# Another order of the work ahead of the second expert: a stencil step and a mixture of eight experts on one core

## The reference

```
h      = layernorm over the features * ln_g + ln_b
h_norm = (h - mean over the tokens) * rsqrt(variance over the tokens + 1e-8), per batch
hyp    = relu(emb[id] @ hyp_w1 + b) @ hyp_w2 + b
sty    = relu(hyp @ sty_w1 + b) @ sty_w2 + b      # gamma (softplus) and beta, per batch
h      = h_norm * gamma + beta
probs  = softmax(h @ router_w); the two largest of 8, rescaled, are the gates
y      = sum over 8 experts of gate_e * (relu(h @ w1_e + b1_e) @ w2_e + b2_e)
out    = x + y
```

## Time and profile before

| | |
|---|---|
| median of 3 runs | 125.39 us (124.72 to 126.44) |
| the profiled execution | 124.87 us |
| its span, first to last instruction | 123.1 us |
| TensorE busy | 113.3 us, 92% of the span |
| VectorE busy | 92.6 us, 75% |
| ScalarE busy | 74.4 us, 60% |
| GpSimd busy | 9.3 us, 8% |
| granted clock of TensorE, mean | 0.986 of full |
| bytes moved | 10.86 MB |

### The profile page before, as it was taken

How to read it: one execution, slowest core, us unless ns; L and a number is a source line. 1 busy time by engine, 2 the same in 40 slices (tenths; PEclk the granted TensorE clock), 3 DMA queues, 4 the chain that set the end, 5 groups by cost and what they waited for, 6 DMA issues and landing times.

```text
span 123.1 us, 1525 instructions
## 1 busy us (share of the span) xinstructions
PE 113.3 (92%) x509; PEld 85.8 (70%) x509; DVE 92.6 (75%) x200; ACT 74.4 (60%) x97; POOL 9.3 (8%) x18
## 2 busy tenths in 40 slices
PE   6899995994699999999999999999999999999970
PEld 2398692442247668888888888888888888888850
DVE  0588749699902839699995996799499679969781
ACT  0403525862041399788888767888887678888900
POOL 1458330000000000000000000000000000000040
PEclk9999999999679999999999999999999999999999
DMA  3999990000000007304050031005002200400004
GB/s 88 300 358 418 418 374 8 0 0 0 0 0 0 0 11 218 123 16 162 0 170 0 0 125 48 0 5 170 0 0 96 75 0 0 170 5 0 0 0 170
DMA packets 4583, 10.86 MB, mean 88 GB/s; under 512 B 800, under 2 KB 1888, under 8 KB 4576
## 3 DMA queue, kind: packets, MB, share of 16 engines
q1 hardware_dynamic: 3920, 9.93, 22.5%
q10 hardware_dynamic: 656, 0.84, 2.4%
HBM read 10.21 MB, written 0.56 MB: 87 GB/s over the span
## 4 chain that ended last, share of the span: by engine, by line
PE 82%; DVE 9%; DMA 3%; ACT 2%; issue 1%; DVEq 0%
PE zt L621 11%; PE zt L622 10%; PE zt L623 10%; PE zt L610 6%; PE aux L645 6%; PE aux L646 6%; PE aux L649 6%; PE yt L645 5%; PE yt L649 5%; PE yt L646 5%; DMA first<-d_difference_dt_ids_dram 3%; PE yt L615 3%; PE zt L539 2%; DVE st L816 1%; PE aux L602 1%
## 5 line engine op out<-in xcount | busy, mean ns | idle before, releaser
L498 ACT ACTIVATE hid_hi<-zt,pv 128x1024 fp32r<-128x1024 f32 x27 | 30.2, 1119 | 16.2 <-PE zt L623 16.1
L937 DVE TENSOR_TENSOR hid_lo<-hid,hid_hi 128x1024 fp32r<-128x1024 f32 x27 | 33.0, 1221 | 8.9 <-issue 5.4
L503 ACT ACTIVATE hid<-zt,pv 128x1024 f32<-128x1024 f32 x27 | 29.9, 1109 | 0.0
L621 PE MATMUL zt<-h_hi,ws 128*128 128x512 f32 x56 | 22.7, 406 | 0.0
L622 PE MATMUL zt<-h_hi,ws 128*128 128x512 f32 x56 | 21.8, 390 | 0.0
L623 PE MATMUL zt<-h_lo,ws 128*128 128x512 f32 x56 | 21.8, 389 | 0.0
L610 PE MATMUL zt<-h,we 128*128 128x512 f32 x16 | 8.9, 708 | 4.0 <-DVE h L845 2.8
L621 PEld LDWEIGHTS zt<-h_hi,ws 128*128 128x128 f32 x56 | 10.5, 188 | 2.9 <-issue 0.5
L622 PEld LDWEIGHTS zt<-h_hi,ws 128*128 128x128 f32 x56 | 10.5, 188 | 2.5 <-issue 0.5
L623 PEld LDWEIGHTS zt<-h_lo,ws 128*128 128x128 f32 x56 | 10.5, 188 | 2.2
L646 PE MATMUL aux<-hid_hi,ws 128*128 128x512 f32 (+1 forms) x32 | 12.0, 376 | 0.0
(11 more groups left out here) (135 smaller groups left out, 146.8 us busy)
## 6 DMA issues: line engine op xcount, KB each, us to landing
we<-in_exp_w_dram SPq DMA_DIRECT2D x8, 512.0 KB, 9.6
gate_all<-gates_dram SPq DMA_DIRECT2D x8, 512.0 KB, 3.6
f<-in_x_dram SPq DMA_DIRECT2D x2, 256.0 KB, 4.9
ft<-in_x_exchanged_dram ACTq DMA_DIRECT2D x2, 256.0 KB, 5.4
out_dram<-acc SPq DMA_DIRECT2D x1, 256.0 KB, 2.0
out_dram<-acc SPq DMA_DIRECT2D x2, 128.0 KB, 2.0
first<-d_difference_dt_ids_dram ACTq DMA_DIRECT2D x1, 136.0 KB, 3.8
gn<-in_grids_dram SPq DMA_DIRECT2D x1, 128.0 KB, 3.8
```

The costliest lines, as they stand in the source:

```text
L498: act.activation(hid_hi[:, c, :], zt[c % 2][:], ACT.Relu, bias=bias).then_inc(hi_ready, 1)
L503: act.activation(hid[:, c, :], zt[c % 2][:], ACT.Relu, bias=bias).then_inc(hid_ready, 1)
L621: pe.matmul(zt[c % 2][:, tok], w_hi, h_hi[:, tok], start=True, stop=False)
L937: v.tensor_tensor(hid_lo[:, c, :], hid[:, c, :], hid_hi[:, c, :].bitcast(F32), ALU.subtract).then_inc(lo_ready, 1)
```

## The change

Nothing that is computed changes, and no instruction is added to the real work. The order of the four lists does.

- **TensorE.** `step_cross`, `rows_b` and `columns_w` of half 1 are cut into pairs of batches. The six warm matmuls between the net's layers are gone; the pairs stand there instead. `columns_b(1)` moves behind `norm_transposed(0)`. The warm matmuls ahead of the first expert are seven instead of six, and no longer wait for `beta` first; two new ones stand ahead of the second half of expert 0. The logits of half 0 are computed ahead of these, those of half 1 behind `layer1_0(1, 0)`.
- **PSUM.** The logits go to the second half of `yt` instead of the first of `aux`, so the wait for `ld` stands ahead of `layer2_0(1, ...)` instead of expert 1's second layer.
- **ScalarE.** `relu_step(2)` runs ahead of `hyper_first`, `inverse_sd_features(0)` ahead of `style_first`, `inverse_sd_features(1)` ahead of `hidden0(0, 1)`. It takes two batches of `h` of half 1 (`H_DVE` is (2, 2) instead of (2, 4)).
- **VectorE.** `split_weights(1)` moves from behind `normalise(1)` to behind `router_start`.
- **GpSimd.** `u_b0` of half 1 comes first of the three products instead of last.

```diff
-WARM_NET = 2
-WARM_H = 6
+WARM_H = (7, 2)
-H_DVE = (2, 4)
+H_DVE = (2, 2)
-        lg_ps = aux[:, half(0)]
+        lg_ps = yt[:, half(1)]
...
             pool.wait_ge(s_ready[1], 1)
+            pool.wait_ge(f_in[1], 16)
+            pool.wait_ge(gn_in, 16)
+            product(u_b0, f, gn[:, 1, :]).then_inc(b0_ready[1], 1)
             pool.wait_ge(ft_in[1], 16)
             pool.wait_ge(gt_in, 16)
             product(u_a1, ft, gt[:, 1, :]).then_inc(a1_ready[1], 1)
             product(u_b1, ft, gt[:, 0, :]).then_inc(b1_ready[1], 1)
-            pool.wait_ge(f_in[1], 16)
-            pool.wait_ge(gn_in, 16)
-            product(u_b0, f, gn[:, 1, :]).then_inc(b0_ready[1], 1)
...
             embedded()
             relu_step(0)
+            relu_step(2)
             hyper_first()
-            relu_step(2)
             hyper_second()
+            inverse_sd_features(0)
             style_first()
-            inverse_sd_features(0)
             normalise(0)
...
             hidden0(0, 0)
+            inverse_sd_features(1)
             hidden0(0, 1)
-            inverse_sd_features(1)
             normalise(1)
...
             transposed_step(1)
+            conditioned(1)
             hidden0(1, 0)
...
             net_layer(0, pw[0:NS, EMB_AT:EMB_AT + SE], onehot[:], SE)
-            keep_warm(WARM_NET)
+            step_cross(1, 0)
             net_layer(1, pw[:, HW1_AT:HW1_AT + SH], se[:], SH)
-            step_cross(1)
+            step_cross(1, 1)
+            rows_b(1, 0, start=True)
             pe.wait_ge(p128_in, 16)
             net_layer(2, pv[:, HW2_AT:HW2_AT + SH], hyp1[:], SH)
-            keep_warm(WARM_NET)
+            rows_b(1, 1, start=True)
             net_layer(3, pv[:, SW1_AT:SW1_AT + SE], hyp2[:], SE)
-            keep_warm(WARM_NET)
+            columns_w(1, 0, final=False)
             pe.wait_ge(net_sb, 4)
...
-            rows_b(1, start=True)
-            columns_b(1)
-            columns_w(1, final=False)
+            columns_w(1, 1, final=False)
             pe.wait_ge(ident_in, 16)
             pe.wait_ge(xp_ready, BH)
             norm_transposed(0)
+            columns_b(1)
             step_transposed(0)
             rows_a(1, start=False)
 
-            pe.wait_ge(net_sb, 6)
-            keep_warm(WARM_H)
+            keep_warm(WARM_H[0])
             wait_for_h(0)
...
             step_transposed(1)
+            logits(0)
+            keep_warm(WARM_H[1])
             wait_for_h(1)
             for c in range(C):
                 if c == C - 1:
                     pe.wait_ge(acc_ready, HALVES)
                 layer1_0(1, c)
-            logits()
+                if c == 0:
+                    logits(1)
+            pe.wait_ge(ld_ready, 1)
             for c in range(C - 1):
                 layer2_0(1, c)
...
             normalise(1)
-            split_weights(1)
             moved = token_stats(1)
             scale_and_shift(1, moved)
             conditioned(1)
             input_parts()
             router_start()
+            split_weights(1)
```

More of the change, by code:

```diff
@@ L533, in net_layer, with of_pair, step_cross @@
                 pe.matmul(small[0:rows, 0:B], weights, acts, start=True, stop=True).then_inc(net_ps, 1)
-            def step_cross(n):
+            def of_pair(n, k):
+                return range(n * BH + 2 * k, n * BH + 2 * k + 2)
+            def step_cross(n, k):
                 pe.wait_ge(s_ready[n], 1)
-                for b in range(n * BH, (n + 1) * BH):
+                for b in of_pair(n, k):
                     last = pe.matmul(one_batch(zt[1], b), s_b2[:, b, :], diff, start=True, stop=True)
-                last.then_inc(rT_ready, 1)
+                if k == 1:
+                    last.then_inc(rT_ready, 1)
             def rows_a(n, start):
@@ L550, in rows_a, with rows_b @@
                         last.then_inc(df_ready, 1)
-            def rows_b(n, start):
+            def rows_b(n, k, start):
                 pe.wait_ge(b0_ready[n], 1)
[L555 to L558, removed]
+                b = n * BH + 2 * k
+                pe.matmul(pair_of(n, k), neg_half_diff2, u_b0[:, b:b + 2, :].rearrange("p b j -> p (b j)"),
+                          start=start, stop=False, skip_group_check=True)
             def columns_b(n):
@@ L564, in columns_b, with columns_w @@
                     pe.matmul(own(b), u_b1[:, b, :], neg_half_diff2, start=False, stop=False, skip_group_check=True)
-            def columns_w(n, final):
+            def columns_w(n, k, final):
                 pe.wait_ge(w_op_ready, n + 1)
-                for b in range(n * BH, (n + 1) * BH):
+                for b in of_pair(n, k):
                     last = pe.matmul(own(b), wT[:, b, :], diff, start=False, stop=final, skip_group_check=True)
-                    if final and b % 2 == 1:
-                        last.then_inc(df_ready, 1)
+                if final:
+                    last.then_inc(df_ready, 1)
             def step_transposed(n):
@@ L597, in wait_for_h, with logits @@
                     pe.wait_ge(h_act_ready, BH * (n + 1) - sum(H_DVE[:n + 1]))
-            def logits():
-                for b in range(B):
+            def logits(n):
+                for b in range(n * BH, (n + 1) * BH):
                     last = pe.matmul(lg_ps[:, b * E:(b + 1) * E], one_batch(h, b), pv[:, RW_AT:RW_AT + E],
@@ L657, in layer2 @@
                     if c == 0:
-                        if e == 1:
-                            pe.wait_ge(ld_ready, 1)
-                        else:
+                        if e > 1:
                             pe.wait_ge(yg_half, HALVES * (e - 2) + min(p, 1) + 1)
@@ L683, in _ @@
             pe.wait_ge(first_in, 16)
-            step_cross(0)
+            step_cross(0, 0)
+            step_cross(0, 1)
             rows_a(0, start=True)
             pe.wait_ge(diff2_in, 16)
-            rows_b(0, start=False)
+            rows_b(0, 0, start=False)
+            rows_b(0, 1, start=False)
             columns_b(0)
-            columns_w(0, final=True)
+            columns_w(0, 0, final=True)
+            columns_w(0, 1, final=True)
             pe.wait_ge(onehot_ready, 1)
@@ L869, in router_start @@
             def router_start():
-                v.wait_ge(logits_ready, 1)
+                v.wait_ge(logits_ready, HALVES)
                 lg = lg_ps[:, 0:B * E].rearrange("p (b e) -> p b e", e=E)
```

## The result

The changed kernel takes 119.66 us in the median of four runs (119.40 to 119.71), the kernel before 125.13 in four (124.72 to 126.44). The ratio is 0.954, 95% interval 0.947 to 0.962: faster by 4.6%. The forecast was 119.8.

The account below looks back on a forecast made before the run. TensorE bounds 82% of the span; experts 1 to 7 are fixed and only their start moves. Gains 2.1 + 0.5 + 0.5 + 1.6 + 0.85 = 5.6 us; 125.4 - 5.6 = 119.8 us, 8-in-10 range 118.6 to 121.8.

Parts of the forecast that it names:

- The block: Experts 1 to 7, from the first matmul of `layer1(1, 0)`: fixed length; only its starting moment can move.
- Part 1, the head: Up to the first L610: earlier roots and reordered TensorE queue start it at 19.1 instead of 21.21; gain 2.1 us.
- is at `norm_transposed(0)` at about 14.45: In the head, after the last net layer: TensorE has only `columns_w(1, 1)` left before half 0's transposes, formerly at 16.75.
- POOL's `u_a1`: In the head, input of `cross_operand(1)`: now POOL's second product instead of first, costing nothing or 0.1 us.
- Part 2, the split: Expert 1's weight split, moved from ahead of `token_stats(1)`: `st` of half 1 at 26.92 instead of 27.46; gain 0.5 us.
- is worth nothing: ScalarE's earlier root of half 1: no gain, as `xn` was already ahead of TensorE.
- Its new place: The split behind `router_start`, where VectorE idled 5.03 us: weights ready by 35.2, TensorE there at 37.9; no cost.
- Part 3: `h` of half 1, two tiles each on VectorE and ScalarE: 0.91 us to L610 instead of 1.43; gain 0.5 us.
- Part 4: TensorE's idle time ahead of half 1: full clock gains 1.6 us on eight passes; half of `logits` off the path, 0.85.
- The clock did not fall again: Rival ahead of half 1: light transposes and logits let the clock fall again, costing 1.6 us, 121.4 us; chance 13%.
- The head gave most of its gain: Rival that the head gives little: late products or waits lose one product's time, 121.1, or all 2.1, 121.9 us; 10%.
- The net without its six warm matmuls: Rival in the head: the level falls to half near 10 us until L610, 127.0 us, slower by 1.3%; chance 3%.

Follow-up runs that it names:

- those with the gap filled: The kernel before with eleven more warm matmuls, or 22 f32 transposes, ahead of the wait for h of half 1: medians 123.54 and 123.70 us.

## Why the prediction was right

**The block.** From L621 to the end 81.6 us in both traces. Right.

**Part 1, the head.** 1.64 us, of 2.1 forecast; 1.9 once the inputs' arrival, 0.26 us later in this execution, is taken off. The step that was too good is "is at `norm_transposed(0)` at about 14.45": TensorE came at 15.09. Of these 0.64 us, 0.26 are the inputs' arrival, the rest is the pairs. I had put a pair at 0.46 us, half of a group in a dense row. The chain of waits of the kernel after (start us, us, what) has 0.64 us for a pair of 128 x 128 between or behind the net's layers, and 0.89 for a whole group of eight passes in a row:

```profile
9.43 0.89 PE yt L574 x8
...
11.49 0.64 PE zt L543 x4
...
13.43 0.64 PE aux L574 x4
...
14.61 0.64 PE aux L574 x4
```

TensorE, not VectorE's `u_a`, still set the start of `st` (0.20 us of waiting on TensorE), if barely. The mechanism stands: TensorE's queue was the bound, and the root matters only once that is lifted, 0 alone and 0.45 behind it. POOL's `u_a1` cost nothing, `tg` did not wait.

**Part 2, the split.** `st` comes 5.64 us behind the first L610, before 6.25: 0.6, forecast 0.5. One sentence was true only of the changed kernel, that the earlier root of half 1 "is worth nothing". With the split in its old place it is worth 0.3 us: `st` comes 5.96 us behind the first L610 in the run with the split put back. So the split's move is worth 0.3 us on top of the root; without the root it would be 0.6, worked out from the same rows, which no run has by itself. Its new place is covered, as forecast: the parts of the weights are there at 33.4 and TensorE comes to them at 35.76, 2.3 us in hand where 2.7 were forecast (the six passes of L615 take 2.2 us by their starts, not 2.7).

**Part 3.** 0.91 instead of 1.43, 0.52; confirmed by undoing it.

**Part 4.** Logits 0.90, forecast 0.85. The passes gave 1.48, forecast 1.6, between these two traces; cut in two by the logits they take 3.59 us by their starts, where the eight in one row at 19.57 take 3.51. But I read the fall of the clock as a fixed property of the kernel before, where one profiled execution showed it. It comes in only a part of its executions: the one of TensorE's order alone idled as long and kept its level, and 9 of 23 runs of before are as fast as those with the gap filled. So the gain, by the stages of the traces, is 3.7 us against an execution without a fall, and 5.2 against one with it. The profiled execution before has the fall, and the median of before lies in the upper group, and so the sum came out near. Had they been from the lower group, the rows would have shown no fall and the forecast would have been reckoned from another base.

**The sum.** It has 5.6 us, the two traces 5.2: the head gave 0.5 less, the rest 0.1 more. For the profiled execution it gave 119.3, measured 119.71. The median of before lay 0.5 above its profiled run, and adding that made up for the 0.4. The mechanism of every part held; that 119.8 met 119.66 so closely is luck.

**The rivals.** The clock did not fall again ahead of the last matmul in any trace of the changed kernel, nor by the mean clock (0.997 or more) in any of its ten runs. With less work in the gap it did fall in some (1 of 4 without the two warm matmuls, 2 of 4 with the logits back), so this rival was a real one. The head gave most of its gain. The net without its six warm matmuls kept its level: the page shows no slice below the highest tenth before the last one.

## What to carry to other kernels

Read who holds a transfer of work between engines before moving anything: an earlier result is worth nothing while the reader is busy with its own queue, and its worth appears only when that queue is put in order. Fillers that only keep the clock up can often be real work cut in pieces, but a small matmul between dependent layers costs more than its share of a dense row. A row that shows a fallen clock tells what an idle stretch can cost, not that it does so each time; look for two groups in the times of the runs and in their mean granted clocks.

## What the hardware showed that I had not expected

- The same idle time of TensorE, 2.75 us, was followed by level 0.50 in two profiled executions (the kernel before, and the one with ScalarE's order alone) and by level 1.00 in a third. The cost in time is 1.5 us.
- 22 transposes of f32 kept the level up in ten of ten runs.
- The runs of the kernel before form two groups on one chip, 123.4 to 124.1 us at a mean clock of 0.992 or more and 124.8 to 126.0 at 0.986 or less, and the share of each differs between chips.
- A pair (four passes) of the 128 x 128 products between two net layers takes 0.64 us in the chain of waits, where a whole group of eight passes takes 0.89.
